# Time mixing of a decoder layer: the receptance input is mixed by ScalarE and GpSimd instead of folded into the weights, and VectorE's shift moves ahead of the states

## The reference

```python
shifted = jnp.concatenate([jnp.zeros_like(x[:, :1, :]), x[:, :-1, :]], axis=1)
xk = x * time_mix_k + shifted * (1.0 - time_mix_k)
xv = x * time_mix_v + shifted * (1.0 - time_mix_v)
xr = x * time_mix_r + shifted * (1.0 - time_mix_r)
k = jnp.einsum('bsd,ed->bse', xk, Wk)
v = jnp.einsum('bsd,ed->bse', xv, Wv)
r = jax.nn.sigmoid(jnp.einsum('bsd,ed->bse', xr, Wr))
wkv = _wkv(k, v, time_decay, time_first)
out = jnp.einsum('bsd,ed->bse', r * wkv, Wo)
```

## Time and profile before

| | |
|---|---|
| median of 3 runs | 3021.46 us (3018.62 to 3022.26) |
| the profiled execution's own time | 3021.09 us |
| its span, first to last instruction | 3019.4 us |
| TensorE busy in the span | 2686.9 us (89%) |
| VectorE busy | 2105.2 us (70%) |
| ScalarE busy | 1815.0 us (60%) |
| GpSimd busy | 743.2 us (25%) |
| mean granted TensorE clock | 0.957 of full |
| time mixing, first to last instruction | 1518.7 to 1995.5 us |

### The profile page before, as it was taken

The page is one execution under the profiler, slowest core; times in us unless marked ns, Lnnn a source line. Parts: engine busy times, 40 slices in busy tenths (PEclk is TensorE's granted clock), DMA queues, the critical chain, the costliest instruction groups (busy, mean ns, idle before and its releaser), DMA issues. The chain is left out here.

```text
span 3019.4 us, 57693 instructions
## 1 busy us (share of the span) xinstructions
PE 2686.9 (89%) x20790; PEld 2002.4 (66%) x20807; DVE 2105.2 (70%) x3830; ACT 1815.0 (60%) x3003; POOL 743.2 (25%) x717
## 2 busy tenths in 40 slices
PE   8999889997888799999969999968898988849899
PEld 6777654553777688888957888845555555525587
DVE  5666648888332232111149999969999999979899
ACT  3333357786222122222247787759999999969886
POOL 0111104445455100010155555122122222020000
PEclk9999989998798899999979999979999999979999
DMA  7000052221455544444421111011101111016676
GB/s 247 1 1 1 32 193 80 86 85 54 150 192 192 188 142 143 145 139 143 155 76 41 37 43 41 10 30 29 27 26 28 30 30 29 16 72 266 235 233 201
DMA packets 135669, 291.87 MB, mean 97 GB/s; under 512 B 21520, under 2 KB 58384, under 8 KB 130832
## 3 DMA queue, kind: packets, MB, share of 16 engines
q1 hardware_dynamic: 117360, 235.29, 23.9%
q0 software_dynamic: 18080, 53.50, 5.4%
HBM read 184.90 MB, written 103.81 MB: 96 GB/s over the span
## 5 line engine op out<-in xcount | busy, mean ns | idle before, releaser
L1331 ACT ACTIVATE cx_h<-bank,early_b 128x256 f32<-128x256 f32 (+1 forms) x288 | 117.6, 460 | 388.4 <-PE bank L1283 388.4
L2050 DVE TENSOR_SCALAR e_low<-bank 128x2048 f32<-128x2048 f32 x128 | 293.4, 2292 | 28.0 <-PE bank L1934 28.0
L1283 PE MATMUL bank<-cx_zT,cx_w 128*128 128x256 f32 (+1 forms) x1152 | 250.1, 371 | 2.1 <-DMA cx_w<-cw_dram 1.3
L1916 ACT ACTIVATE e_low<-e_low 128x2048 f32<-128x2048 f32 x128 | 244.9, 1913 | 4.1
L1294 PE MATMUL bank<-early_w,cx_h 128*128 x1088 | 246.6, 379 | 0.0
L1914 ACT ACTIVATE e_low<-e_low 128x2048 f32<-128x2048 f32 x128 | 243.6, 1903 | 0.0
L1283 PEld LDWEIGHTS bank<-cx_zT,cx_w 128*128 128x128 f32 x1152 | 212.0, 192 | 30.3 <-DMA cx_w<-cw_dram 1.7
L1294 PEld LDWEIGHTS bank<-early_w,cx_h 128*128 128x128 f32 x1088 | 201.2, 190 | 24.4
L1934 PE MATMUL bank<-e_qT,e_kT 32*128 32x256 f32 x2048 | 147.4, 401 | 66.9 <-DVE e_high L2051 66.1
L1346 DVE COPY cx_zT<-bank 128x512 f32<-128x512 f32 (+1 forms) x72 | 47.7, 662 | 202.7 <-PE bank L1274 202.7
L1354 DVE TENSOR_TENSOR cx_y<-bank,early_b 128x512 f32<-128x512 f32 (+1 forms) x72 | 47.7, 662 | 198.7 <-PE bank L1294 198.7
(11 more groups left out here) (392 smaller groups left out, 6740.8 us busy)
## 6 DMA issues: line engine op xcount, KB each, us to landing
cx_w<-cw_dram SPq DMA_DIRECT2D x72, 512.0 KB, 3.6
hidden<-fu_h SPq DMA_DIRECT2D x32, 1024.0 KB, 3.8
fd_h<-hidden SPq DMA_DIRECT2D x64, 512.0 KB, 4.2
cx_rows<-expert_rows SPq DMA_DIRECT2D x64, 256.0 KB, 3.5
slot_y<-cx_y POOLq DMA_DIRECT2D x64, 256.0 KB, 2.6
early_ctx_first<-ctxT_dram SPq DMA_DIRECT2D x32, 256.0 KB, 6.1
queries<-g_qT SPq DMA_DIRECT2D x32, 256.0 KB, 5.3
b_qT<-queries SPq DMA_DIRECT2D x32, 256.0 KB
```

Of the source, the lines that this page charges most:

```text
L1283: last = nc.tensor.matmul(H[k][f // 2][:, (f % 2) * GROUP_ROWS:(f % 2) * GROUP_ROWS + cols], w1[k][:, c, f * P:(f + 1) * P], zT[k][:, c, 0 ...
L1916: nc.scalar.activation(flat(low[n % RING][:]), flat(low[n % RING][:]), ACT.Exp, scale=-1.0).then_inc(low_ready, 1)
L2050: nc.vector.tensor_scalar(flat(low[n % RING][:]), HEADS4.rearrange("p r s -> p (r s)"), -1.0, 0.0, ALU.mult, ALU.max).then_inc(neg_ready, 1)
```

## The change

It has three pieces.

1. Receptance is no longer projected from `zT` with two sets of weights. ScalarE, right behind the copy `turned(b)`, multiplies `zT` columns 1 to 256 by mix and columns 0 to 255 by 1-mix (`part`, 4 instructions of 128x256, L1569 and L1570 of the new text), GpSimd adds the two products (`mix`, one instruction of 128x512, L1524), and TensorE projects the sum with the plain weights: 8 rows of MATMUL in place of 16.
2. GpSimd's loop runs gather(b), mix(b-4), collect(b-1), and goes on to round 35.
3. On VectorE `centre(b+4)` stands between gates(b-1) and states(b) and no longer behind weigh(b-1). The weights of receptance are not premixed (4 instructions less at the start).

```diff
--- before.py
+++ after.py
@@ -1458,8 +1458,9 @@
         sb = lambda n, shape, dt=FP: ctx.enter_context(nc.sbuf_tensor("d_" + n, shape, dt))
         TWO, RING, AHEAD = range(2), 3, 4
         w = [sb(f"w{m}", [P, DC, D]) for m in "kvr"]
-        now = [sb(f"now{m}", [P, DC, D]) for m in "kvr"]
-        before = [sb(f"before{m}", [P, DC, D]) for m in "kvr"]
+        now = [sb(f"now{m}", [P, DC, D]) for m in "kv"]
+        before = [sb(f"before{m}", [P, DC, D]) for m in "kv"]
+        part = [[sb(f"part{k}{p}", [P, DC, S]) for p in range(2)] for k in range(2)]
         wo, cols = sb("wo", [P, DC, D]), sb("cols", [P, 5, DC])
         rest, wcol, limit, neg_limit = sb("rest", [P, 3, DC]), sb("wcol", [P, DC]), sb("limit", [P, DC]), sb("neg_limit", [P, DC])
         shift, decay = sb("shift", [P, NT]), sb("decay", [P, DC, S])
@@ -1476,9 +1477,9 @@
         nd, whole = sb("nd", [P, 2, DC, S]), sb("whole", [P, DC, S])
         gate, y = sb("gate", [P, DC, S]), [sb(f"y{k}", [P, DC, S]) for k in TWO]
         names = ("cols_in", "setup", "wexp", "consts", "weights", "shift", "z", "zT_raw", "zT", "k_raw", "v_raw", "r_raw", "pp", "h", "arg", "ex", "abs", "er",
-                 "ev", "state", "prod", "nd", "whole", "ln", "gate_in", "gate", "y", "o_raw", "x_done", "first", "second", "weighed", "pool_first", "pool_second", "spread", "moments", "log_var", "rstd")
+                 "ev", "state", "prod", "nd", "whole", "ln", "gate_in", "gate", "y", "o_raw", "x_done", "first", "second", "weighed", "part", "mix", "pool_first", "pool_second", "spread", "moments", "log_var", "rstd")
         (cols_in, setup, wexp, consts, weights, shift_ready, z_ready, zT_raw, zT_ready, k_raw, v_raw, r_raw, pp_ready, h_ready, arg_ready, ex_ready, abs_ready, er_ready,
-         ev_ready, state_ready, prod_ready, nd_ready, whole_ready, ln_ready, gate_in, gate_ready, y_ready, o_raw, x_done, first_in, second_in, weighed, pool_first, pool_second, spread_ready, moments_ready, log_var_ready, rstd_ready) = (sem(n) for n in names)
+         ev_ready, state_ready, prod_ready, nd_ready, whole_ready, ln_ready, gate_in, gate_ready, y_ready, o_raw, x_done, first_in, second_in, weighed, part_ready, mix_ready, pool_first, pool_second, spread_ready, moments_ready, log_var_ready, rstd_ready) = (sem(n) for n in names)
         chosen_in, w_in = [sem(f"chosen_in{k}") for k in range(RING)], [sem(f"w_in{m}") for m in "kvro"]
         K, V, R, T = bank[0:2], bank[2:4], bank[4:7], bank[7]
         halves = lambda b: b[:].rearrange("p (c s) -> p c s", c=DC)
@@ -1508,7 +1509,7 @@
                 pool.wait_ge(pool_first, b - AHEAD + 1)
                 nc.gpsimd.tensor_tensor(x, x, chosen_y[b % RING][1][:], ALU.add).then_inc(pool_second, 1)
 
-            for b in range(B):
+            def gather(b):
                 if b >= AHEAD + RING:
                     pool.wait_ge(pool_second, b - RING - AHEAD + 1)
                 elif b >= RING:
@@ -1517,9 +1518,18 @@
                     for n in range(TB):
                         pool.indirect_dma_start(chosen_y[b % RING][c][:, n, :], None, t["slot_y"],
                                                 bass.IndirectOffsetOnAxis(ap=t["slot"][:, c, b * TB + n:b * TB + n + 1], axis=0)).then_inc(chosen_in[b % RING], 16)
-                if b > AHEAD:
+
+            def mix(b):
+                pool.wait_ge(part_ready, 2 * DC * (b + 1))
+                nc.gpsimd.tensor_tensor(part[b % 2][0][:], part[b % 2][0][:], part[b % 2][1][:], ALU.add).then_inc(mix_ready, 1)
+
+            for b in range(B + AHEAD):
+                if known(b):
+                    gather(b)
+                if known(b - AHEAD):
+                    mix(b - AHEAD)
+                if AHEAD < b <= B:
                     collect(b - 1)
-            collect(B - 1)
 
         @block.scalar
         def _(act):
@@ -1554,6 +1564,10 @@
                 if b > 1:
                     act.wait_ge(r_raw, b - 1)
                 nc.scalar.activation(zT[b % 2][:, :, 1:S + 1], halves(T), ACT.Copy).then_inc(zT_ready, 1)
+                act.wait_ge(zT_ready, b + 1)
+                for c in range(DC):
+                    nc.scalar.activation(part[b % 2][0][:, c, :], zT[b % 2][:, c, 1:S + 1], ACT.Copy, scale=cols[:, 2, c:c + 1]).then_inc(part_ready, 1)
+                    nc.scalar.activation(part[b % 2][1][:, c, :], zT[b % 2][:, c, 0:S], ACT.Copy, scale=rest[:, 2, c:c + 1]).then_inc(part_ready, 1)
 
             def receptance(b):
                 act.wait_ge(r_raw, b + 1)
@@ -1658,10 +1672,14 @@
 
             def receptance(b):
                 if b == 0:
-                    pe.wait_ge(weights, 3 * WEIGHTS)
+                    pe.wait_ge(w_in[2], 16)
                 if b > 2:
                     pe.wait_ge(gate_in, b - 2)
-                project(b, 2, R[b % 3], r_raw)
+                pe.wait_ge(mix_ready, b + 1)
+                for e in range(DC):
+                    for c in range(DC):
+                        last = nc.tensor.matmul(R[b % 3][:, e * S:(e + 1) * S], w[2][:, c, e * P:(e + 1) * P], part[b % 2][0][:, c, :], start=c == 0, stop=c == DC - 1)
+                last.then_inc(r_raw, 1)
 
             def output(b):
                 if b == 0:
@@ -1786,7 +1804,8 @@
             ch.end()
             dve.wait_ge(setup, INIT)
             for b in range(AHEAD - 1):
-                mixed(b)
+                if b < 2:
+                    mixed(b)
                 collect(b)
                 centre(b)
             maxima(0)
@@ -1806,12 +1825,12 @@
                     add(b - 2)
                 if known(b - 1):
                     gates(b - 1)
+                if known(b + AHEAD):
+                    centre(b + AHEAD)
                 if known(b):
                     states(b)
                 if known(b - 1):
                     weigh(b - 1)
-                if known(b + AHEAD):
-                    centre(b + AHEAD)
 
 
 def layer1_stablemax(nc, t, d, bank):
```

## The result

| | before | after |
|---|---|---|
| median, lowest and highest of 5 runs each | 3021.98 us (3018.62 to 3024.76) | 3031.94 us (3027.26 to 3034.2) |
| ratio with its 95% interval | | 1.0028 (1.0016 to 1.0040) |
| profiled execution: own time | 3021.09 us | 3032.26 us |
| profiled execution: span | 3019.4 us | 3030.6 us |

The change made the kernel slower, by 0.16 to 0.40%. The forecast was 3031.

A forecast was written before the change was run, and what follows sets the result against it. VectorE was taken to set the pace in the middle, mean period 13.35 us. Terms of +6 us there, +2 at the start and +1.5 at the end made +9.5, so 3031 us; range 3005 to 3040.

The forecast's parts named there:

- The shift's move: VectorE's two-element shift, moved from behind y to between gates and states, no longer waits for GpSimd: gain 1.07 us a period.
- the free period: VectorE's period where GpSimd adds nothing, 12.31 us, from which the sum for one period starts.
- Y held by the addition: GpSimd's new addition asks during the second scan, goes ahead of y on VectorE: loss 1.09 us a period.
- L1737 held: VectorE's former L1719, two SBUF inputs, waits for GpSimd's later old additions: 0.34 us a period.
- The logarithm's wait: VectorE's wait for ScalarE's logarithm lies under the hold of L1719: 0.16 us a period taken off.
- The start: First rounds: products of batch 1 ahead of ScalarE's first round, 1.8 us; bounds 1.9 less to 5 more, taken as +2.
- the new wait costs TensorE nothing: TensorE's wait for the product sum costs nothing, since the sum is made a whole period ahead of its projection.
- The end: Last rounds, paced by TensorE at 12.39 us: two still hold an addition, some 13.2, two don't, 12.2; +1.5 us.
- The sum: Whole stage: +6 us in 24 middle periods, +2 at the start, +1.5 at the end, in all +9.5 us.
- No collision for y: Rival: GpSimd's addition doesn't hold y or y goes first; period 12.45 us, time 3001; chance 0.22.
- Clearly slower: Rival: GpSimd's additions hold further VectorE instructions, 0.5 to 1.1 us a period each; 14 us on top, 3045; chance 0.07.
- The clock: Rival: TensorE falls to half clock after waits; mild form costs nothing, severe some 200 us more, chance 0.01.

The follow-up runs named there:

- shift-alone run: Kernel before with only the shift moved ahead of the states, no mix on ScalarE and GpSimd: 2940.29 against 2949.76 us, ratio 0.9964.
- second chip: Changed kernel run once more, against the kernel before on the same chip: 2963.23 against 2948.35 us, ratio 1.0052.
- first pair: Kernel before and changed kernel as first measured for the result: 3031.94 against 3021.98 us, ratio 1.0028.
- mended order: Changed kernel's operations reordered, early batches' sums and products moved, ScalarE's gates and scaling ahead of the zT copy; against kernel before: 2929.58 against 2948.35 us, ratio 0.9938.
- mix alone: Changed kernel with the shift left behind y, against the kernel before: 2974.86 against 2949.76 us, ratio 1.0082.

## Why the forecast came out

**The shift's move, a gain of 1.07 us a period.** Right in the instruction (1.23 to 0.15). As a gain by itself it is 0.37, because L1719 is then held by 0.33 and TensorE leaves no round below 12.84; beside the mix it is 13.95 - 13.455 = 0.50. My sum started from the free period of 12.31 and never needed it alone.

**Y held by the addition, 1.09.** Right, and the mechanism is as told: the addition asked during the second scan, at 0.50 us from its start. From y's start to that of the next instruction it was 0.59 us and is 1.62 (1710.00 to 1711.62): 1.03. L1524 took 1.77 us, within the 1.3 to 1.9 foretold, and y ended 0.55 us behind it, as foretold. The rule that whoever asks first goes next holds with this lead of 0.62 us; with one of 0.01 to 0.02, in the shift-alone run, it doesn't.

**L1737 held, 0.34.** Right: 1.56 in place of 1.22.

**The logarithm's wait, 0.16.** Too small. From the statistics of X to the gates it was 0.90 us in the free period and is 0.67: 0.23. So 12.31 + 1.03 + 0.34 - 0.23 = 13.45. I had 13.58. Over 24 or 25 rounds the difference to before is +2.6 to +2.9 us and not +6: this term was mis-sized, by two errors of 0.06 and 0.07 us that a difference of two large terms multiplies.

**The start, +2.** On the execution of the result it was 0.3 + 2.2 = 2.5 us, close to the forecast. On the second chip it was 5.0 + 2.2 = 7.2, beyond the upper bound of 5, and there the step in the forecast fails. I had counted the products (1.8, measured 1.7) and had not followed the addition through: GpSimd's queue puts it behind gathers, receptance waits for it, and on TensorE the transposition of the next batch is queued behind receptance. I said that "the new wait costs TensorE nothing"; in the steady state that holds, in the first round it doesn't. That the 5.0 are the addition's is shown by the run without it, which has 46.1 us to the first `whole` and not 51.4. In the first pair an unexplained later start covers the loss, which the forecast did not foresee.

**The end, +1.5.** 0.9. The rounds were 13.10, 13.14, 13.14 and then 12.12, as foretold in shape.

**The sum.** 9.5 were forecast for the stage. In the pair that gave the result it is 4.0 by the profiles (2.5 at the start, 1.2 in the 25 rounds, 0.9 at the end, less 0.5 behind the last `whole`), and 5.7 without the clock's 1.7 in the kernel before. The medians differ by 9.96 us, 4.8 to 12.1 by the interval, and 7.2 of the 11.2 us between the profiled executions lie outside the stage. On the second chip the stage gives 11.0 and the medians 14.9. So 3031 against 3031.94 is luck to a good part: the mechanism of the middle is right, its size is half of what I wrote, and time that the sum doesn't treat of made up for it.

**The rivals.** *No collision for y* didn't happen: the addition led by 0.62 us. Its price of 12.45 us a period wasn't tested. The mended order comes to 12.50, but with y still at 0.98 and in another sequence, and with y freed in the changed order itself the round is 13.55. The Trainium skill, Perfetto Trace Analysis, Optimizing Scalar/DVE Operations, says that a 2-port VectorE operation holds the port it shares with GpSimd; read as the two-port modes alone, that would leave y at 0.67 us. It took 1.70, so that reading doesn't fit this trace. *Clearly slower* (the former L1721 held too) shows in the run with the addition behind y, L1741 at 2.19 us, where other holds had gone. *The clock* stayed at its full 2.4 GHz (1.00 in the stretch above) with 17 us of idle time in 100; TensorE's waits in the middle were at most 1.66 us. The mild form of this rival did appear in other runs, where TensorE waited 2.1 to 2.7 us for VectorE: with the addition behind y nothing was lost, as foretold, and in the run without the addition some 6 us, by the estimate above. At the changed kernel's start on the second chip it may have a share that wasn't tested: from 1480 to 1530 us the granted clock is 0.80 in the mean, and 0.93 in the kernel before.

What wasn't tried: two additions of half the size on GpSimd in place of one, which could fit smaller stretches.

## What to carry to other kernels

An operation given to GpSimd isn't free when VectorE sets the pace: look for the instruction of VectorE with two SBUF inputs that runs when the addition asks, and count 1.0 to 1.1 us for it in each period, the price in this kernel. Give each addition a stretch of VectorE's order in which one input comes from PSUM or there is one input only, and make it by the order of the program on both engines. And follow each new wait through the first round by itself, with all that is queued behind it, before the period is multiplied. When two profiles are compared, look at the granted clock round by round first: one stretch of 3.4 us at half clock was followed here by a single round 1.7 us longer.

## What the runs showed of the hardware

- **What excludes what.** Over the twelve profiles and this stage, VectorE's instructions with two inputs in SBUF were longer than their usual time by over 0.25 us 485 times, and each time an addition of GpSimd ran beside them. Instructions with one input, or with one in PSUM, took no longer beside an addition than without: the scan of the maxima 0.69 us at most in 629 cases beside one and in 81 without, statistics 0.43 at most in 137 and in 1209.
- **TensorE's clock fell around waits of 2.1 to 2.7 us.** In the middle of the stage (the second to the 26th round) each fall to 1.2 GHz, 3.4 us long, came with such a wait for VectorE; many rounds with the same wait passed without one. In the changed kernel, with 1.66 us at most, none came. In the run without the addition and in the first profile of the kernel before, the round after a fall was 0.9 to 1.7 us longer; in the mix alone and with the addition behind y no round was.
- **Who goes first is decided within hundredths of a microsecond.** In the shift-alone run the row of GpSimd's addition begins 0.01 to 0.02 us before y's 25 times, and y went first each time (0.66 to 0.67 us). With a lead of 0.06 us (1799.51 and 1799.57 above) GpSimd went first, and the two-element shift took 1.23 us. Between 0.02 and 0.06 no case was seen.
- **GpSimd gets in between two VectorE instructions that follow without a gap.** Its addition then ends about 1.1 us after the one that ran has ended (1711.15 against 1710.09 above), and VectorE's next one goes on from there.
- **The first indirect gather after the additions** takes 1.77 us to issue and not 0.95, where it begins beside L1737:

```profile
1714.33 1.77 POOL L1519 DMA_INDIRECT d_chosen<-slot_y,slot  x1
...
1716.40 0.95 POOL L1519 DMA_INDIRECT d_chosen<-slot_y,slot  x1 [0.30 <-issue]
```

Those that begin beside VectorE's statistics take 0.95. Over the twelve profiles all 269 gathers that begin beside that first instruction of `ratio` take more than 1.0 us, and 224 of 255 that begin beside the second one, with two SBUF inputs as well, don't: what decides between these two wasn't tested.
